# A vision tower in groups of four images: the second FFN layer in blocks of 128 tokens instead of 112

## The reference

```python
pooled = x.reshape(Bb, Cc, n, K, n, K).sum(axis=(3, 5))
h = jnp.einsum('bcij,ce->bije', pooled, channel_weights)          # 64 x 196 x 192
h = h + attn(layernorm(h))       # y = x.at[idx].add(gated[idx]) for 14 tokens an image
t = layernorm(h)
h = h + gelu(t @ in_weight.T + in_bias) @ out_weight              # 192 -> 768 -> 192, for all tokens
```

## Time and profile before

| | |
|---|---|
| median of 3 runs | 670.09 us (669.08 to 673.85) |
| profiled execution | 671.92 us |
| its span | 670.2 us |
| mean granted TensorE clock | 0.949 |
| busy share of the span: TensorE, its loads, VectorE, ScalarE, GpSimd | 88%, 71%, 76%, 52%, 36% |
| HBM | 171.82 MB, 256 GB/s over the span |
| L715, second layer f32 | 1344 matmuls, 266.6 us, 336 ns each |
| L1055, sums of x | 111 instructions, 258.8 us |
| L893, Gelu | 192 instructions, 95.3 us, 497 ns each |

### The profile page before, as it was taken

One profiled execution on the slowest core, in us unless ns is written; L12 is line 12 of the kernel. 1 busy time (PEld: TensorE's weight loads), 2 busy tenths in 40 slices (PEclk: granted clock), 3 DMA queues, 4 the chain that ended last, 5 costly groups with the idle time before them and its releaser, 6 DMA issues.

```text
span 670.2 us, 12462 instructions
## 1 busy us (share of the span) xinstructions
PE 590.3 (88%) x3912; PEld 474.7 (71%) x3912; DVE 508.6 (76%) x1110; ACT 347.2 (52%) x847; POOL 242.1 (36%) x458
## 2 busy tenths in 40 slices
PE   2568687999998999899979979989989999999995
PEld 1346374777977797768767867769777877788774
DVE  4988669797979797979888866979897888752411
ACT  2013325475656556655656445656565565646541
POOL 1022333151545245443626224533634273304001
PEclk9886586999999999999999979999999999999998
DMA  8999958889898969897897869797999884010101
GB/s 320 332 384 366 400 160 326 288 289 309 283 354 277 353 231 366 266 358 243 322 308 282 260 229 295 256 355 240 361 271 342 257 334 95 10 41 12 32 6 42
DMA packets 33461, 171.82 MB, mean 256 GB/s; under 512 B 3428, under 2 KB 17776, under 8 KB 20978
## 3 DMA queue, kind: packets, MB, share of 16 engines
q1 hardware_dynamic: 21600, 146.11, 60.4%
q0 software_dynamic: 6512, 11.01, 9.1%
q10 hardware_dynamic: 5282, 13.87, 5.6%
HBM read 158.55 MB, written 12.43 MB: 255 GB/s over the span
## 4 chain that ended last, share of the span: by engine, by line
PE 44%; DVE 19%; issue 12%; DMA 9%; POOL 8%; ACT 5%; POOLq 1%; SPq 1%; DVEq 0%; ACTq 0%
PE psO L715 16%; DVE R L1055 5%; DMA X<-in_x 5%; PE psS L670 4%; PE psF L700 3%; PE psS L647 3%; DMA patch_sums<-R 3%; PE psS L659 3%; PE psC L685 2%; PE psC L690 2%; PE psA L613 2%; DMA out<-OS,idx 2%; DVE mx L1169 2%; PE psS L653 2%; ACT SP L830 1%
## 5 line engine op out<-in xcount | busy, mean ns | idle before, releaser
L715 PE MATMUL psO<-W,act 128*112 128x192 f32 x1344 | 266.6, 336 | 7.0 <-ACT act L893 7.0
L1055 DVE TENSOR_REDUCE R<-X 128x42 f32<-128x2688 f32 (+1 forms) x111 | 258.8, 2358 | 18.2 <-POOL X L430 16.6
L715 PEld LDWEIGHTS psO<-W,act 128*112 128x112 f32 x1344 | 217.4, 180 | 25.6 <-issue 17.8
L893 ACT ACTIVATE act<-psF 128x392 f32<-128x392 f32 x192 | 95.3, 497 | 134.8 <-PE psF L700 122.1
L430 POOL TENSOR_TENSOR X<-X 128x1344 f32<-128x1344 f32 x31 | 93.9, 3032 | 13.5 <-DMA X<-in_x 13.5
L700 PE MATMUL psF<-Stk,M1S 104*128 104x392 bf16 x192 | 65.9, 343 | 8.5 <-ACT act L893 8.5
L439 POOL TENSOR_TENSOR Pt<-Praw 48x196 f32<-48x196 f32 x14 | 7.5, 536 | 153.2 <-DMA Praw<-patch_sums 153.2
L900 ACT ACTIVATE obuf<-psO 112x192 f32<-112x192 f32 x112 | 36.6, 326 | 27.8 <-PE psO L719 23.4
L659 PE MATMUL psS<-ET,F 98*64 98x336 f32 x128 | 41.9, 472 | 1.5 <-ACT ET L873 1.5
L700 PEld LDWEIGHTS psF<-Stk,M1S 104*128 104x128 bf16 x192 | 18.9, 99 | 32.9 <-ACT act L893 24.8
L670 PE MATMUL psS<-B,G 128*56 128x192 f32 x192 | 41.0, 337 | 0.0
(11 more groups left out here) (225 smaller groups left out, 929.4 us busy)
## 6 DMA issues: line engine op xcount, KB each, us to landing
X<-in_x SPq DMA_DIRECT2D x96, 1344.0 KB, 8.0
X<-in_x SPq DMA_DIRECT2D x15, 672.0 KB, 4.4
X<-in_x POOLq DMA_DIRECT2D x15, 672.0 KB, 13.5
out<-obuf ACTq DMA_DIRECT2D x16, 588.0 KB, 8.4
patch_sums<-R ACTq DMA_DIRECT2D x14, 147.0 KB, 8.4
Praw<-patch_sums ACTq DMA_DIRECT2D x14, 147.0 KB, 5.5
act<-in_x SPq DMA_DIRECT2D x1, 1344.0 KB, 18.7
W1T<-in_w1t SPq DMA_DIRECT2D x1, 576.0 KB
```

The costliest lines, as they stand in the source:

```text
L715: pe.matmul(to, act_sb[u % 2][:, m, i * OT:(i + 1) * OT], W2[:, m, :], start=(m == 0), stop=False)
L893: act.activation(act_sb[u % 2][:, n // 2, (n % 2) * (GT // 2):(n % 2 + 1) * (GT // 2)], psF[:, 0:GT // 2], ACT.Gelu).then_inc(act_F1.sem, 1)
L1055: dve.tensor_reduce(R[:, r, t * TQ * N:(t + 1) * TQ * N].rearrange("p (q j) -> p q j", q=TQ), v, AX.XY, ALU.add).then_inc(dve_L, 1)
```

## The change

The second layer takes blocks of 128 tokens, six a group: 768 tokens. The 16 tokens left over of an even group and the 16 of the next odd one share a block of 32 rows (number 12 of the pair's 13), with the small output tile out_left, which two small transfers of 12 KB store. To bring the left tokens together, ScalarE copies their Gelu outputs into act_left (step l:0, after the last Gelu) and each stack copy becomes two instructions. In an even period the steps o:6.* and O:6 do nothing; in an odd one they do the shared block. The store of the six blocks (576 KB) is issued at O:5. A row of obuf is now 6 successive tokens.

```diff
-FT = 7
-FP = T // FT
-OT = GB * FP
+FT = GB * T // 128
+OT = 128
+WHOLE = FT * OT
+LEFT = GB * T - WHOLE
+NB = 2 * FT + 1
@@ sync, gpsimd
+            sp.wait_ge(y_left, NG // 2 * 32)
                 pool.wait_ge(y_out[e], landed(g, e))
+                pool.wait_ge(y_left, q * 32 + 32)
@@ tensor: step_F2
+                j = block_of(u, i)
+                rows = OT if i < FT else 2 * LEFT
+                to = psO[(u // 2 + j) % 2][0:rows, 0:D]
...
+                    elif i == FT:
+                        pe.wait_ge(act_F1.sem, act_F1.at(g, "left"))
+                    if j >= 2:
+                        pe.wait_ge(act_F2.sem, act_F2.at(q, f"o{j - 2}"))
+                    elif exists(g - 2):
+                        pe.wait_ge(act_F2.sem, act_F2.at(q - 1, f"o{j - 2 + NB}"))
                 if m < HT:
+                    rows_in = act_sb[u % 2][:, m, i * OT:(i + 1) * OT] if i < FT else act_left[:, m, u // 2, :]
+                    pe.matmul(to, rows_in, W2[:, m, :], start=(m == 0), stop=False)
...
+                            if u % 2 or int(step[0]) < FT:
+                                step_F2(g, u, pair_of(i, k, lag), int(step[0]), m)
@@ scalar
+            def copy_stack(to, left):
+                tokens = psA[:, :].bitcast(bf16)[0:SK, 0:GT]
+                act.activation(by_block(to), tokens_by_block(tokens), ACT.Copy)
+                act.activation(left, tokens[:, WHOLE:GT], ACT.Copy).then_inc(act_K.sem, 1)
...
+            def gather_left(g, u):
+                act.wait_ge(act_F1.sem, act_F1.at(g, f"n{NF1 - 1}"))
+                at = LEFT * (u % 2)
+                act.activation(act_left[:, :, u // 2, at:at + LEFT], act_sb[u % 2][:, :, WHOLE:GT], ACT.Copy).then_inc(act_F1.sem, 1)
...
+                if i == FT:
+                    if exists(g - 2):
+                        act.wait_ge(y_left, q * 32)
+                    act.activation(out_left[:, :], bank[0:2 * LEFT, 0:D], ACT.Copy).then_inc(act_F2.sem, 1)
+                else:
+                    act.activation(obuf[u % 2][:, i, :], bank[0:OT, 0:D], ACT.Copy).then_inc(act_F2.sem, 1)
+                if i >= FT - 1:
+                    act.wait_ge(act_F2.sem, act_F2.at(q, f"o{j}"))
                 if i == FT - 1:
-                    act.wait_ge(act_F2.sem, act_F2.at(g, f"o{i}"))
-                    act.dma_start(og[bass.ds(g, 1)].rearrange("o p q -> (o p) q"),
+                    act.dma_start(og[bass.ds(g, 1), 0:WHOLE, :].rearrange("o (p i) e -> (o p) (i e)", i=FT),
                                   obuf[u % 2][:, :, :].rearrange("p i e -> p (i e)")).then_inc(y_out[u % 2], 16)
+                elif i == FT:
+                    for e in range(2):
+                        act.dma_start(left_of(g - 1 + e), out_left[e * LEFT:(e + 1) * LEFT, :]).then_inc(y_left, 16)
...
-                    "f:10:1 O:6:2 f:11:1 C:gb:2 S:e0:1 S:e1:1 S:e2:1 S:e3:1 S:e4:1 S:e5:1").split()
+                    "f:10:1 O:6:2 f:11:1 C:gb:2 l:0:1 S:e0:1 S:e1:1 S:e2:1 S:e3:1 S:e4:1 S:e5:1").split()
```

More of the change, by code:

```diff
@@ L175, in program @@
         act_sb = [sb(f"act{i}", [128, HT, GT]) for i in range(2)]
+        act_left, stk_left = sb("act_left", [128, HT, 2, 2 * LEFT]), sb("stk_left", [SK, 2, 2 * LEFT], bf16)
         ZY = sb("ZY", [FR, SLOTS])
@@ L218, in program @@
         y_out = [sem(f"out_stored{k}") for k in range(2)]
+        y_left = sem("left_tokens_stored")
         scat = [sem(f"chosen_stored{k}") for k in range(2)]
@@ L249, in program @@
         ffn = " ".join(f"n{k}" for k in range(NF1))
-        outs = " ".join(f"o{k}" for k in range(FT))
+        outs = " ".join(f"o{k}" for k in range(NB))
         pe_F1 = Steps(sem("pe_ffn1"), ffn)
-        act_F1 = Steps(sem("act_gelu"), ffn)
+        act_F1 = Steps(sem("act_gelu"), ffn + " left")
         pe_F2 = Steps(sem("pe_ffn2"), outs)
```

54 lines of the change are left out of this document (31 added, 23 removed).

## The result

The changed kernel takes 683.3 us (median of four runs, 676.0 to 685.5) beside 671.97 us for the kernel before on the same chip: 1.0141 times as long, with an interval of 1.0095 to 1.0186. The prediction said 674.7 (667 to 681). It is slower by more than 1%, and above the range. Measured twice more, it took 679.9 and 681.0 us, at the upper end of the range.

The account below looks back on a forecast made before the run. It took even periods to end when VectorE, not TensorE, is ready. Terms 0 - 0.3 + 2.3 + 1.5 + 1.0 + 0.1 = +4.6 us made 676.5 for the profiled run, 674.7 in the median (667 to 681).

Parts of the forecast that it names:

- The block removed: Block gone from even groups: 0 us gained in 7 even periods, which VectorE ends; other bound the whole 2.13 each.
- The rival that came true: the clock: TensorE, idle some 4 of 32.8 us in even periods, loses clock: 6.9 us more, 681.6; chance 0.04.
- the end of the kernel: Last even period: softmax earlier, -0.3 us (0 to -0.67); last two stores before the last Gelu: +0.1.
- The small stores: Odd periods: second store issue, 0.40 us, delays last Gelu; 0.33 a period after slack, 2.3 in all (1.8 to 3.8).
- The second stack copies: Each stack copied in two ScalarE instructions; TensorE waits 0.1 us longer, 15 periods: 1.5 us (0 to 3.0).
- Wider weights: Weight loads of 128 columns instead of 112, 191 ns not 180, about 6 times a period: 1.0 us (0 to 2.1).
- The forecast's 4.6: Sum of all terms over the whole kernel, +4.6 us, added to the profiled execution's 671.92.
- The stall of the negation: VectorE's negation held until GpSimd's halving ends, 1.24 us against a median of 0.17; gone or doubled meant wrong.
- The rival of the load that moves: Big store delays the load ahead of GpSimd's halving: 679.6 if by 0.7 us, 668.8 if beyond 1.8; chance 0.14.
- the one in which TensorE is the bound: Removed block counts in full if VectorE's product comes 0.76 us sooner in even periods: -12.1, 658.0; chance 0.08.
- The one in which the costs are hidden: Second store issue and second stack copy overlap other waits or matmuls, only 1 us left: 671; chance 0.19.

Follow-up runs that it names:

- e13: The changed kernel as it is, third measurement: 680.95 us, 1.0146 of the kernel before, clock 0.936.
- e14: The changed kernel plus four unread matmuls in one of three emptied gaps of even periods, beside the changed kernel's third measurement: 672.52 us, 1.0023, clock 0.953.
- e12: The changed kernel plus four unread matmuls in one of the three emptied gaps of even periods, first measurement: 672.71 us, 1.0035, clock 0.955.
- e1: The changed kernel plus twelve unread matmuls, filling all three emptied gaps of even periods: 677.01 us, 1.0075, clock 0.952.
- e2: The kernel before, without the twelve f32 matmuls of block 6 in even groups: 674.89 us, 1.0060, clock 0.936.
- e7: The kernel before, with the negation of the score maxima done by ScalarE instead of VectorE: 669.05 us, 0.9967.
- e4: The kernel before, with weight tiles of 128 columns for the first six blocks of each group: 672.60 us, 1.0030.
- e10: The kernel before, plus a second ScalarE copy of 16 columns behind each of the two stack copies: 674.24 us, 1.0050.
- e6: The changed kernel with twelve unread matmuls in the gaps and both small stores issued after the last Gelus and the gather: 676.00 us, 1.0062.
- e5: The changed kernel as it is, second measurement: 679.93 us, 1.0121 of the kernel before, clock 0.935.
- e3: The changed kernel with both small stores issued after the last Gelus and the gather: 676.28 us, 1.0119, clock 0.937.
- e9: The kernel of e6, with the shared block multiplying 128 columns of other tokens instead of the 32 left ones: 672.89 us, 1.0039.
- e11: The kernel before, without the twelve f32 matmuls of block 6 in odd groups: 676.15 us, 1.0110, clock 0.928.

## Why the prediction was wrong, step by step

**The step that failed.** The sum had no term for TensorE's clock. It took the removed block for free work in gaps and left out what the work did for the clock, and the rival that had it got 0.04. The runs show 8.4 us in its place (e13 against e14), of the 9.6 by which the changed kernel is slower there. With some or all of the gaps filled the kernel takes 672.5 to 677.0 us (e14, e12, e1), inside the range.

**The block removed: right.** The prediction took 0 for the even periods. Where the clock held, the period is 32.96 us against 32.77 for its like before, TensorE is busy 29.30 (forecast about 29), A:zt waits 1.75 for VectorE (about 1.7), and f:8 and f:9 are 0.93 apart. e2 and e7 show it by experiment: work taken from TensorE gives next to nothing (0.35 us in an even period whose clock held), and work taken from VectorE does.

**The rival that came true: the clock.** It was named, and its time, 681.6, is within 2 us of the three medians measured (683.3, 679.9, 681.0); by its own factors it is 681.4, since 7 x 16 x 0.06 is 6.7 and not 6.9. What failed is its chance of 0.04, and the sentence that gave it: the rows don't show a fall for gaps this short, because an even stretch with 1.9 us idle had a clock of 1.00. That stretch had its gaps filled with thirds of block 6; the changed one has two waits of 0.59 us one behind the other with 0.34 us of matmul between them. The total idle time of a period, 1.9 or 4 us, was the wrong measure. What should have been drawn is the row of instructions left after the removal: at f:7 to f:9 TensorE works 0.34 of every 0.93 us. The Trainium skill (TensorE: Matmul & The Clock Gate, the section on a second failure mode with the queue of PSUM banks) describes a kernel whose clock goes up and down because TensorE idles briefly and often between groups of matmuls. The trace agrees: 0.59 us of idleness, repeated, and 4.14 us for 2.24 us of work behind it. The prediction cited the page for idle stretches and passed over this section.

The size was near by luck. The prediction spread 6.9 us evenly over half of seven even periods. In the profile, the long fall costs 4.6 us and the short one at 202 us 0.6; a third, at 349 us, stands in a period that is 0.3 to 0.4 longer than in e14 and e12. A fall in an odd period costs more, because there is no wait to take it up. The period from 434.10 to 474.03 has a clock of 0.96 and lasts 39.93 us, 2.5 more than the same one before (37.44). There the fall comes behind a wait of f:6 for Gelu. Its row in TensorE's timeline, and a row of the windows a little later:

```profile
455.74 0.34 PE L715 MATMUL psF<-Stk,M1S 104*128 104x392 bf16 x1 [0.85 <-ACT act L924]
```

```profile
458.00:460.00 2.00, 2.00 (x8) 0.58 1.02 357
```

That place is not one that the change emptied: before, the same wait of f:6 was 1.20 us long, and the clock held. The removed block isn't needed for this fall: the same period has a clock of 0.92 in e4 and 0.96 in e10, where the block is there, and 0.92 in e6 and e12, where gaps are filled. So these 2.5 of the 13.5 us between the two profiles don't belong to the removed block.

And the end of the kernel, for which -0.3 + 0.1 was forecast, took 4.7 us more. TensorE at the end of the kernel before:

```profile
656.63 0.38 PE L679 MATMUL psC<-K,xh 120*96 120x120 f32 x2 [1.10 <-DVE xh L1204]
...
661.72 2.21 PE L690 MATMUL psC<-W,actS 128*120 128x192 f32 x12 [0.45 <-ACT actS L885]
```

And of the changed one:

```profile
639.54 0.51 PE L715 MATMUL psF<-Stk,M1S 104*128 104x392 bf16 x1 [0.59 <-ACT act L924]
639.85 3.53 PE L662 MATMUL psS<-FM,UB 120*112 120x196 f32 x12
...
666.93 0.38 PE L694 MATMUL psC<-K,xh 120*96 120x120 f32 x2 [0.99 <-DVE xh L1258]
...
673.80 3.65 PE L705 MATMUL psC<-W,actS 128*120 128x192 f32 x12 [1.82 <-ACT actS L916]
```

From the last A:zt to xh it is 51.53 us instead of 50.03: +1.5, with the fall at f:8 again (3.53 for the scores). From xh to the last group of matmuls it is 6.87 instead of 5.09: +1.8, for the two small stores stand ahead of the last Gelu. From there to the end it is 9.90 instead of 8.48: +1.4, because the wait of 1.82 us for that Gelu is followed by matmuls at the lower clock, 3.65 us instead of 2.21. The forecast had 0.1 for the stores and nothing for the clock. In e12 and e14 this last part is 64.1 us, 0.5 to 0.6 above the one before.

**The small stores: right in kind, too small in size.** The prediction took 0.40 us for the second issue, so 0.73 for both. ScalarE's timeline of the changed kernel, with the stores of one odd period and those at the end:

```profile
242.52 0.32 ACT L943 ACTIVATE out_left<-psO 32x192 f32<-32x192 f32 x1 [0.35 <-PE psO L742]
242.87 1.93 ACTq L953 DMA_DIRECT2D out<-out_left  x2
244.84 0.50 ACT L924 ACTIVATE act<-psF 128x392 f32<-128x392 f32 x1 [2.00 <-issue]
...
671.29 2.06 ACTq L953 DMA_DIRECT2D out<-out_left  x2
```

A pair takes 0.81 us at best, and 1.93 and 2.06 here: of the 16 issues the median is 0.34 us and the longest 1.69. After a pair of 0.83 us (at 538.82) o:0.0 waits 0.47 us for the last Gelu, forecast about 0.3; after the one of 1.93 it waits 1.22. What makes an issue long isn't shown by these rows. In the medians the stores are hard to see, as said. The traces give them a size. These are the five odd periods that have a clock of 1.00 in all the traces named (the 1st, 2nd, 3rd, 6th and 7th of a trace), added up, and how much longer they are than the same five before:

| kernel | us more than before, in five periods |
|---|---|
| changed (first trace, e5, e13) | 3.6, 3.8, 3.5 |
| changed with gaps filled (e1, e14) | 5.0, 4.7 |
| stores late (e3, e6) | 1.5, 1.7 |
| stores late, no narrow tile (e9) | 0.5 |
| before with small copies (e10) | 0.4 |
| before with wider tiles (e4) | 0.0 |

So the stores are the largest cost of the work: 2 to 3.3 us in five periods, 0.4 to 0.7 each, where the prediction had 0.33.

**The second stack copies.** The odd period at 507 us:

```profile
519.56 0.81 ACT L871 ACTIVATE Stk<-psA 104x768 bf16<-104x768 bf16 x1 [0.87 <-PE psA L628]
520.26 0.18 ACT L872 ACTIVATE stk_left<-psA 104x16 bf16<-104x16 bf16 x1
```

The first copy ends at 520.37, the second at 520.44, and A:sl starts at 520.50, 0.06 after it: the delay is 0.07 us, forecast 0.1. By the median of e10 the term is 3.4 us instead of 1.5; as said, its trace shows only a part, some 0.07 us an odd period.

**Wider weights: not shown to cost anything.** By the median it is 2.0 us (e4) instead of 1.0, in a forecast range of 0 to 2.1, but the interval begins at 0 and the odd periods of the trace are no longer than before. The narrow tile's 0.1 us a third was no term at all: 0.3 x 7 = 2 us.

**What the work of the change costs stays open.** With the clock kept, the medians give different answers: 1.2 us (e14), 2.3 (e12: 0.0035 of 671), 6.0 (e1), and 4.4 with the stores late (e6). Measured one by one, copies, widths, stores and narrow tile make 3.4 + 2.0 + 1.0 + 2 = 8.4 us, each with an uncertainty of about 2 us. The forecast's 4.6 lies between, and no run shows it too high or too low. The traces show one thing that speaks against the cost and that neither the prediction nor a run looked for: TensorE's stall between the two halves is shorter. TensorE's idle time in it is 4.4 to 4.7 us in the five traces whose blocks are those before (4.49 in the profile before), and 0.9 to 3.3 in all eleven with blocks of 128 tokens; in e2 and e11, which leave work out of the kernel before, it is 3.35 and 0.92. As an estimate from these rows: seven odd periods at 0.7 us each are 5 us, the shorter stall gives back 1.2 to 3.6, and what is left, 1.4 to 3.8 us, is about what e14 and e12 show. What sets the length of the stall isn't known.

**The stall of the negation went, but not by the load.** The prediction named a stall that is gone as a sign of being wrong. Before, five of the 16 negations take from 0.75 to 2.18 us, 8.6 in all; in the changed kernel two do, 4.5 in all. The load isn't why. GpSimd's halving begins 26.0 to 28.5 us into these five periods before and 26.2 to 27.8 after. The three stalls that are gone are those of the periods in which the clock fell at the scores or just before: there the negation came later. Where the clock held it is as in the earlier trace rows. The changed kernel's VectorE has:

```profile
502.11 1.19 DVE L1226 TENSOR_SCALAR nm<-mx 112x6 f32<-112x6 f32 x1
```

and its GpSimd:

```profile
500.26 3.02 POOL L444 TENSOR_TENSOR X<-X 128x1344 f32<-128x1344 f32 x1
```

They end at 503.30 and 503.28. In e12 and e14, whose clock held there, all five stalls are back (7.5 and 7.6 us in all). The rival of the load that moves, with its 0.14, is out. So is the one in which TensorE is the bound (0.08). The one in which the costs are hidden (671, 0.19) comes near e14's 672.5 us in its number but not in its reason: the costs show in the odd periods, and a shorter stall makes up for part of them.

## What to carry to other kernels

A matmul that fills a wait can cost next to no time, and yet be what keeps TensorE at its higher clock level. Before taking work out of TensorE, look at what ends its waits in that stretch: if it isn't TensorE, the removal buys little, and the clock may fall in the row of instructions that is left (here 0.34 us of work in every 0.93, twice), which then also slows the stretch that is dense. Where that happens, shorten the chain that TensorE waits for, or leave something in one of the gaps, and measure again with the granted clock beside every run.

## What the runs showed of the hardware that was not expected

- The clock fell where no wait was longer than 0.59 us: in the fall at 202.3 us two such waits stand behind f:7, and the scores after them take 3.84 us instead of 2.24. Four matmuls of 192 columns in one of the two places prevent it there (no fall at this place in e12 and e14; mean clock 0.953 against 0.936, 8.4 us).
- Equal periods of one execution differ: with the same work and the same gaps, the even periods of the changed kernel have 1.00, 0.95 or 0.82. What decides which wasn't found; it makes one kernel's runs spread from 676.0 to 685.8 us, in the order of their clocks (0.942 to 0.930).
- A kernel with 16 us less matmul work and nothing added is 0.6% slower (e2), and 1.1% slower where the work is taken out of odd periods (e11).
- Slower matmuls don't lengthen a period by their whole delay: scores that were 1.60 us longer cost 0.56, since VectorE's negation then came after GpSimd's instruction and took 0.17 us instead of 1.19.
- A weight tile of 32 columns doesn't hide behind a first-layer matmul: what follows starts 0.26 us after that matmul, not 0.17.
- Issuing a small store from ScalarE takes 0.34 us in the median, but up to 1.69 when two follow each other.
- TensorE stands still once between the two halves of the steady part, waiting for nothing that the profile shows, for 0.9 to 4.7 us by the kernel.
